# A two-layer graph attention kernel: one sign in eight of two granules made on VectorE, and a new order of work between the layers

## The reference

```python
# layer 1
src = h @ a1; dst = h @ a2
e = leaky_relu(src[:, None] + dst[None, :], 0.01)
e = where(adj > 0, e, NEG_INF)
x = layernorm(x + softmax(e, axis=1) @ h)
# layer 2, on the x of layer 1
wh = x @ weight_w
e = leaky_relu((wh @ a_src)[:, None] + (wh @ a_dst)[None, :], 0.01)
e = where(adj > 0, e, NEG_INF)
x = layernorm(x + softmax(e, axis=1) @ wh + bias)
```

## Time and profile before

| | us |
|---|---|
| median of three runs | 491.33 |
| lowest, highest | 489.75, 494.29 |
| the profiled execution | 490.02 |
| its span, first to last instruction | 487.6 |
| TensorE busy in the span | 435.6 (89%) |
| VectorE busy | 413.6 (85%) |
| ScalarE busy | 394.3 (81%) |
| GpSimd busy | 85.3 (18%) |

### The profile page before, as it was taken

One profiled execution on the slowest core, in us unless ns is written; L12 is line 12 of the kernel. 1 busy time (PEld: TensorE's weight loads), 2 busy tenths in 40 slices (PEclk: granted clock), 3 DMA queues, 4 the chain that ended last, 5 costly groups with the idle time before them and its releaser, 6 DMA issues.

```text
span 487.6 us, 11722 instructions
## 1 busy us (share of the span) xinstructions
PE 435.6 (89%) x4409; PEld 411.8 (84%) x4409; DVE 413.6 (85%) x751; ACT 394.3 (81%) x586; POOL 85.3 (18%) x59
## 2 busy tenths in 40 slices
PE   0799858998988989899998997989999999999993
PEld 0379757987988889899888986989999999999993
DVE  3789998889989898989989997999677786967776
ACT  2685188778897888779889918999999999999940
POOL 0012221512415133151431210001010010101011
PEclk9987979997999979889898988999999999999998
DMA  7999999999999999999994300152130303021100
GB/s 184 255 245 273 273 269 276 330 310 313 326 320 328 308 311 307 311 335 303 321 322 143 130 1 0 58 162 64 36 97 0 97 0 97 11 86 55 42 12 13
DMA packets 83525, 89.27 MB, mean 183 GB/s; under 512 B 7426, under 2 KB 79394, under 8 KB 83490
## 3 DMA queue, kind: packets, MB, share of 16 engines
q1 hardware_dynamic: 48834, 54.57, 39.8%
q10 hardware_dynamic: 34656, 34.21, 25.5%
HBM read 79.32 MB, written 9.45 MB: 182 GB/s over the span
## 4 chain that ended last, share of the span: by engine, by line
PE 42%; DVE 24%; DMA 18%; issue 12%; ACTq 1%; ACT 1%; SPq 1%; POOL 0%; POOLq 0%; DVEq 0%
PE acc L467 40%; DMA stage<-in_adj 17%; DVE narrow L872 5%; DVE turned L884 4%; DVE pos L893 2%; DVE num L987 1%; DMA kept<-in_x 1%; DVE num L994 1%; DVE red L982 1%; DVE kept L794 1%; DVE bn L999 1%; DVE num L984 1%; DVE kept L884 1%; PE flip L393 1%; DVE kept L788 1%
## 5 line engine op out<-in xcount | busy, mean ns | idle before, releaser
L602 ACT ACTIVATE neg<-srow,dcol 128x512 int8<-128x512 f32 (+1 forms) x320 | 222.5, 861 | 11.8 <-issue 8.0
L467 PE MATMUL acc<-xy_old,pos 128*128 128x195 bf16 x1024 | 195.9, 261 | 18.1 <-POOL pos L1143 11.4
L467 PE MATMUL acc<-xy_old,neg 128*128 128x195 bf16 x1024 | 195.7, 261 | 0.0
L467 PE MATMUL acc<-stage,pos 128*128 128x195 bf16 x1024 | 180.6, 250 | 2.6 <-issue 2.6
L467 PE MATMUL acc<-stage,neg 128*128 128x195 bf16 x1024 | 180.5, 250 | 0.0
L602 ACT ACTIVATE neg<-xy_old,dcol 128x512 int8 (+1 forms) x192 | 137.5, 1034 | 0.0
L467 PEld LDWEIGHTS acc<-xy_old,pos 128*128 128x128 fp8e4 x1024 | 106.5, 104 | 26.9 <-issue 25.4
L467 PEld LDWEIGHTS acc<-xy_old,neg 128*128 128x128 fp8e4 x1024 | 105.8, 103 | 1.4
L467 PEld LDWEIGHTS acc<-stage,pos 128*128 128x128 fp8e4 x1024 | 101.7, 99 | 3.4 <-issue 3.0
L467 PEld LDWEIGHTS acc<-stage,neg 128*128 128x128 fp8e4 x1024 | 101.2, 99 | 0.3
L872 DVE TENSOR_SCALAR narrow<-stage 128x4096 uint8<-128x4096 int32 x32 | 74.3, 2320 | 13.1 <-DMA stage<-in_adj 12.2
(11 more groups left out here) (134 smaller groups left out, 345.9 us busy)
## 6 DMA issues: line engine op xcount, KB each, us to landing
stage<-in_adj ACTq DMA_DIRECT2D x64, 512.0 KB, 9.3
stage<-in_adj SPq DMA_DIRECT2D x64, 512.0 KB, 9.2
spill<-turned SPq DMA_DIRECT2D x16, 512.0 KB, 7.7
turned<-spill SPq DMA_DIRECT2D x16, 512.0 KB, 3.7
xy_old<-score_rows SPq DMA_DIRECT2D x6, 256.0 KB, 4.4
out<-x1s SPq DMA_DIRECT2D x7, 128.0 KB, 1.9
xn<-in_x SPq DMA_DIRECT2D x1, 768.0 KB, 16.6
kept<-in_x SPq DMA_DIRECT2D x4, 128.0 KB, 3.9
```

What stands on the lines that cost most here:

```text
L467: last = nc.tensor.matmul(acc[:, r, c * XW:(c + 1) * XW], masks[c][:, t // BYTES, t % BYTES, r * P:(r + 1) * P], xy[layer][:, g * GT + t, ...
L602: last = nc.scalar.activation(o[:, t // BYTES, t % BYTES, :], row, ACT.Sign, bias=dcol[:, layer, col:col + 1])
```

## The change

- VectorE makes tile 7 of granules 1 and 3 of blocks 2 to 7 in layer 2 (`own_sign`): a comparison of the kept row with minus the column score, times 255, written into the same place of `neg`. ScalarE makes seven signs there and eight in granules 0 and 2. `minus_columns` computes the negated scores once. That is 12 comparisons on VectorE and 12 Signs fewer on ScalarE.
- TensorE's order between the layers: (2, 0, 0) is done in two halves, with `project(6)` between them; `score_row(1, 1)` goes behind `turn_x1(7)`; `mean1` goes from ahead of (2, 0, 2) to behind it.
- ScalarE makes the signs of (2, 0, 2) around `copy_x1(7)`, and ahead of `copy_wh(7)`. For this VectorE copies the column scores of supers 4 and 5 early (`columns`).
- `scores1` fills one stretch of PSUM instead of two, and the copy of it is one instruction instead of two.
- VectorE's order in block 1: the read of block 0 goes ahead of mask (1, 1), and mask (1, 2) goes ahead of `add_near` to `moments`. `normalize1(0)` then follows `moments` directly. In the loop the order of the instructions is the same as before, with `own_sign` ahead of the masks of granules 1 and 3, and the loop's seam in another place.

```diff
+    OWN = (None, GT - 1, None, GT - 1)
...
+            granule(1, 0, 0, (0, 1))
+            project(NS - 2)
+            granule(1, 0, 0, (2, 3))
+            turn_x1(NS - 1)
             score_row(1, 1)
-            project(NS - 2)
-            granule(1, 0, 0)
-            turn_x1(NS - 1)
             project(NS - 1)
             turn_max(1)
             spread_max(1)
             granule(1, 0, 1)
             pe.wait_ge(xT_ready, 2 * NS)
-            mean1()
+            pe.wait_ge(shift_ready, 4)
             scores1(NS - 2, NS)
             granule(1, 0, 2)
+            mean1()
...
+                if kept_row and OWN[g] is not None:
+                    tiles = [t for t in tiles if t != OWN[g]]
...
+            signs(1, 0, 2, range(0, 5))
             copy_x1(NS - 1)
+            signs(1, 0, 2, range(5, GT))
             copy_wh(NS - 1)
-            signs(1, 0, 2, range(0, 4))
             act.wait_ge(shift_ready, 4)
             exps(1, slice(NEAR, TILES), minus_shift[:, 1, 0:1], minus_shift[:, 1, 1:2], far_exp)
-            signs(1, 0, 2, range(4, GT))
...
+            def own_sign(s, g):
+                k = (NS + s) * NG + g
+                o = neg[:, g, :].rearrange("p (b i e) -> p b e i", b=GB, e=BYTES)
+                t = OWN[g]
+                dve.wait_ge(products, (k + 1) * RB)
+                dve.sem_inc(dve_turn, 1)
+                row = rows_sb[:, bass.ds(s - 2, 1), :].rearrange("p o n -> p (o n)")
+                nc.vector.tensor_scalar(o[:, t // BYTES, t % BYTES, :], row, minus_dcol[:, g * GT + t:g * GT + t + 1], 255.0,
+                                        ALU.is_lt, ALU.mult).then_inc(own_signs, 1)
+                dve.wait_ge(own_signs, 1 + (s - 2) * (NG // 2) + g // 2 + 1)
...
+            columns(slice(NEAR_SUPS, NS - 2), 2)
             step(weigh(1, 1, rest1))
...
             mask1(1, 0)
             keep_score_rows()
             row_factors1()
+            read_acc(1, 0)
             mask1(1, 1)
-            read_acc(1, 0)
+            mask1(1, 2)
             add_near()
             average(1, 0)
             residual_sum(1, 0)
             moments(1, 0)
-            mask1(1, 2)
             normalize1(0)
+            minus_columns()
+            mask1(1, NG - 1)
...
             with dve.Fori(1, NS - 1) as s:
-                mask1(s, NG - 1)
-                for g in range(NG):
-                    if g:
-                        mask1(s + 1, g - 1)
-                    if g == 1:
-                        read_acc(1, s)
-                    if g == 2:
-                        average(1, s)
-                        residual_sum(1, s)
-                        moments(1, s)
+                mask1(s + 1, 0)
+                read_acc(1, s)
+                mask1(s + 1, 1)
+                average(1, s)
+                residual_sum(1, s)
+                moments(1, s)
+                mask1(s + 1, 2)
                 normalize1(s)
-            mask1(NS - 1, NG - 1)
+                mask1(s + 1, NG - 1)
```

More of the change, by code:

```diff
@@ L150, in gat_kernel @@
         scores = old_f[:, near_end:near_end + IB]
+        minus_dcol = old_f[:, near_end + IB:near_end + IB + TILES]
         raw_near = old_f[:, rows_end:raw_end].rearrange("p (r n) -> p r n", r=RB)
@@ L162, in gat_kernel @@
         s_psum0 = misc[:, 408:408 + IB]
-        s_psum1 = [misc[:, 408:408 + 3 * IB // 4], flip[:, 256:256 + IB // 4]]
+        s_psum1 = misc[:, 408:408 + IB]
         mean_psum = flip[:, 0:BYTES * D]
@@ L204, in gat_kernel @@
         signs_ready = sem("signs_ready")
+        own_signs = sem("own_signs")
         neg_ready = sem("neg_ready")
@@ L407, in scores1 @@
             def scores1(first, end):
-                part = first // (NS - 2)
                 for s in range(first, end):
@@ L411, in scores1 @@
                         b = s * RB + r
-                        last = nc.tensor.matmul(s_psum1[part][:, row_at(s - part * (NS - 2), r)], xT[:, b * P:(b + 1) * P],
-                                                v_src[:, :], start=True, stop=True)
-                if end in (NS - 2, NS):
+                        last = nc.tensor.matmul(s_psum1[:, row_at(s, r)], xT[:, b * P:(b + 1) * P], v_src[:, :],
+                                                start=True, stop=True)
+                if end == NS:
                     last.then_inc(scores_psum, 1)
@@ L591, in signs @@
                     else:
-                        act.wait_ge(dcol_ready, 1 + g // (NG // 2))
+                        act.wait_ge(dcol_ready, max(1, g))
                 act.wait_ge(products, (k + 1) * RB)
@@ L602, in signs @@
                     last = nc.scalar.activation(o[:, t // BYTES, t % BYTES, :], row, ACT.Sign, bias=dcol[:, layer, col:col + 1])
-                if tiles[-1] == GT - 1:
+                if tiles[-1] >= GT - 2 and (kept_row or tiles[-1] == GT - 1):
                     last.then_inc(signs_ready, 1)
@@ L759, in keep_scores @@
             def keep_scores():
-                dve.wait_ge(scores_psum, 4)
-                nc.vector.tensor_copy(scores[:, 0:3 * IB // 4], s_psum1[0])
-                nc.vector.tensor_copy(scores[:, 3 * IB // 4:IB], s_psum1[1]).then_inc(scores_kept, 1)
+                dve.wait_ge(scores_psum, 3)
+                nc.vector.tensor_copy(scores, s_psum1).then_inc(scores_kept, 1)
             def keep_score_rows():
@@ L805, in tables0, with columns @@
                 split(0, g, rest0).then_inc(tables_ready, 1)
+            def columns(supers, n):
+                t = slice(supers.start * BYTES, supers.stop * BYTES)
+                dve.wait_ge(wh_kept, 1 + supers.stop)
+                nc.vector.tensor_copy(dcol[:, 1, t], wh1[:, t, D]).then_inc(dcol_ready, 1)
+                dve.wait_ge(dcol_ready, n)
             def far_columns(n):
                 t = [slice(0, NEAR), slice(NEAR, TILES)][n]
-                dve.wait_ge(wh_kept, 1 + [NEAR_SUPS, NS][n])
-                nc.vector.tensor_copy(dcol[:, 1, t], wh1[:, t, D]).then_inc(dcol_ready, 1)
-                dve.wait_ge(dcol_ready, n + 1)
+                columns([slice(0, NEAR_SUPS), slice(NS - 2, NS)][n], [1, 3][n])
                 nc.vector.tensor_reduce(mcol[:, 4:5], dcol[:, 1, t], AX, ALU.max).then_inc(max_step, 1)
@@ L909, in last_mask0, with minus_columns @@
                 nc.vector.tensor_tensor(c, c, a, ALU.bitwise_and).then_inc(neg_ready, 1)
+            def minus_columns():
+                nc.vector.tensor_scalar(minus_dcol, dcol[:, 1, :], -1.0, None, ALU.mult).then_inc(own_signs, 1)
+            def own_sign(s, g):
[8 more added lines that the diff above has]
+                dve.wait_ge(own_signs, 1 + (s - 2) * (NG // 2) + g // 2 + 1)
             def negative(s, g):
                 k = (NS + s) * NG + g
+                if OWN[g] is not None and not (isinstance(s, int) and s < 2):
+                    own_sign(s, g)
                 dve.wait_ge(signs_ready, k + 1)
@@ L1100, in _ @@
             moments(1, 0)
-            mask1(1, 2)
             normalize1(0)
-            with dve.Fori(1, NS - 1) as s:
-                mask1(s, NG - 1)
-                for g in range(NG):
-                    if g:
-                        mask1(s + 1, g - 1)
-                    if g == 1:
-                        read_acc(1, s)
-                    if g == 2:
-                        average(1, s)
-                        residual_sum(1, s)
-                        moments(1, s)
+            minus_columns()
+            mask1(1, NG - 1)
+            dve.wait_ge(own_signs, 1)
+            for n, rows in enumerate((1, NS - 3)):
+                dve.wait_ge(rows_in[n], 16 * rows)
+            with dve.Fori(1, NS - 1) as s:
+                mask1(s + 1, 0)
[5 more added lines that the diff above has]
+                mask1(s + 1, 2)
                 normalize1(s)
-            mask1(NS - 1, NG - 1)
+                mask1(s + 1, NG - 1)
             for part in HALVES:
```

## The result

The changed kernel takes 494.2 us (median of 17 runs, 492.03 to 496.55), the kernel before in the same comparisons 490.68 us (17 runs). The ratio is 1.0074, 95% interval 1.0054 to 1.0094, which is 3.6 us (2.6 to 4.6) slower. I forecast 2.0 us slower.

A forecast was written before the change was run, and what follows sets the result against it. TensorE was taken to pace blocks 2 to 7, with ScalarE's savings hidden. 490.02 + 0.3 (between the layers and block 1) + 1.7 (loop and tail) = 492.0 us profiled, 493.3 us for the median; range 490.3 to 496.5.

The forecast's parts named there:

- The bound: Layer 2, blocks 2 to 7: TensorE paces at 22.1 us a block, and ScalarE's 8.6 us less work gains nothing.
- ScalarE's pace: Rival, blocks 2 to 7: ScalarE holds TensorE, so 12 fewer Signs bring up to 8.6 us; chance 0.05.
- The 8 us of idle time: Sign of a right forecast: ScalarE idle by some 8 us in blocks 2 to 7.
- Block 1: Layer 2, block 1: stalls of 2.18 and 0.40 us go, a new one of 3.0 us comes ahead of (2, 1, 3).
- GpSimd's power: Block 1, ahead of `normalize1(0)`: the power takes 1.82 us, and VectorE stands still for 2 us.
- TensorE's end of block 0: Layer 2: TensorE ends block 0 at 321.85 as before, with up to 0.4 us more.
- The sum of the whole stretch: Between the layers and through block 1: +0.3 us, from -0.3 at best to +0.8 if the copy is late.
- The comparison: `own_sign` on VectorE in the loop: 0.54 us each, 0.51 for the instruction and 0.03 for the wait until the mask.
- The rival at one element a time: The comparison takes 0.79 us with its wait, so loop and tail cost 3.4 us instead of 1.7; chance 0.12.
- What it exposes: Granule 2's mask, blocks 2 to 7: 0.54 us later against 0.42 slack, so 0.12 us a block exposed, 0.7 in all.
- The clock: Rival: TensorE's clock falls behind the new stall in block 1, costing 1.7 us, to 495.0; chance 0.26.
- Loop and tail: Blocks 2 to 7: 0.7 us for six masks plus 1.0 us ahead of (2, 7, 3), together 1.7 us.

The follow-up runs named there:

- fewer_signs: The kernel before with tile 7's sign left out, not replaced, in granules 1 and 3 of blocks 2 to 7; one execution, 206.3 us from block 6's turn to the end.
- compare_only: The kernel before plus the twelve comparisons, seven Signs in those granules and the moved loop seam, with the old order elsewhere; ratio 1.006.
- after_look1: The changed kernel, unchanged, traced a second time; 210.8 us from the turn of block 6 to the end.
- after_look2: The changed kernel, unchanged, traced a third time; 209.4 us from the turn of block 6 to the end.
- mean_back: The changed kernel with `mean1` put back ahead of (2, 0, 2); ratio 1.0043 to the kernel before.
- mask_first: The changed kernel with the mask of block 1's granule 3 moved ahead of `normalize1(0)` and `minus_columns`; ratio 1.0055 to the kernel before.
- order_only: The changed kernel with no comparison on VectorE and all eight Signs on ScalarE, so only the order differs from the kernel before; ratio 1.0032.
- mask_first_no_compare: The changed kernel with block 1's granule 3 mask ahead of `normalize1(0)` and no comparison on VectorE; ratio 0.9977 to the kernel before.
- before_look1: The kernel before, unchanged, traced a second time; 206.4 us from the turn of block 6 to the end.

## Why the prediction was right or wrong

**The bound: right.** TensorE paces blocks 2 to 7, and ScalarE's 12 Signs fewer are worth nothing there (fewer_signs, compare_only). The rival "ScalarE's pace" is out. The 8 us of idle time I had ScalarE down for came as 2.7 us of waits for TensorE and 4.4 us less from its first Sign of these blocks to its last (133.06 us against 137.47).

**Block 1: the mechanism was right, two sizes were off.** The stalls of 2.18 and 0.40 us went, and one came ahead of (2, 1, 3), released by VectorE's mask. I had 3.0 us, and the three traces show 1.97, 1.49 and 1.50. One size was GpSimd's power: it took 1.01 us instead of the 1.82 of the earlier trace rows, and VectorE waited 1.32 us for it, where I had 2. The other was TensorE's end of block 0, which I had held at its old time. Counted from the turn of block 6 TensorE was ready for block 1 0.4 us later than before in the first trace. There the mask of (2, 1, 2) still waited 0.39 us for ScalarE's Signs, as I had assumed; in the two later traces TensorE ended block 0 so late that the Signs were ready, and the stall was shorter by the difference. The chain of the changed kernel, 335 to 350 us, without its pieces of up to 0.1 us, reads as the list I had written:

```profile
337.56 0.18 DVE small L1029
337.92 1.01 POOL small L1160
339.05 0.20 DVE x1s L1039
339.28 0.75 DVE x1s L1039 x3
340.13 1.14 DVE neg L944
341.29 1.24 DVE pos L949
342.62 7.42 PE acc L469 x84
```

The sum of the whole stretch came to +0.5 us on average (-0.5 to +1.7) for the +0.3 I took, whose range was -0.3 to +0.8. Both ends were missed. At the top is after_look1, which has the low-clock stretch of 1.7 us; after_look2 has it as well and came to +0.3.

**The comparison: 0.516 us measured for 0.51.** The view of the changed line gives least, median and greatest of the twelve in ns:

```profile
L932 DVE TENSOR_SCALAR neg<-xy_old x12: 509/516/525, 348.8 to 472.0; 128x512 uint8 x12
L932 DVEq FUSED_REGOPS  x6: 69/69/69, 348.6 to 460.4; - x6
```

The row for the narrowing of adj, scaled, was the right neighbour. The rival at one element a time is out. The estimate from the Trainium skill, "VectorE: DVE Perf Modes", cycle comparison, 0.42 us, was 0.1 too low; the 0.07 that I had added for the scalar per partition makes up most of that.

**What it exposes: the term that was mis-sized.** I allowed 0.03 us between comparison and mask, as between the two halves of a mask. Behind granule 1's comparison it is 0.13 (348.83 + 0.52 = 349.35 to 349.48), behind granule 3's 0.03 to 0.04. So the mask of granule 2 came 0.65 us later instead of 0.54, and with 0.42 us of slack 0.225 a block were exposed instead of 0.12. For the last granule 3 it is 0.65 + 0.55 = 1.2 instead of 1.08. The six register operations in the rows above stand only at granule 1, once a block. The first begins at 348.6 us, ahead of the comparison at 348.83 and not between it and the mask, so the rows don't show them to be the 0.1 us; its cause stays open.

**The tail: a term that was missing.** 0.34 us come behind the last granule 3. In the changed kernel VectorE pauses between its two statistics instructions in the first half of the last block:

```profile
481.00 0.36 DVE L1026 BATCH_NORM_STATS2 bn<-num 128x6 f32<-128x64 f32 x2
481.86 0.25 DVE L1028 BATCH_NORM_AGGREGATE mv<-bn 128x2 f32<-128x6 f32 x2 [0.51 <-DVE bn L1026]
```

Before, the idle time there was 0.15 us. It is 0.51 in all six traces with two comparisons a block (three of the changed kernel, compare_only, mean_back, mask_first), and 0.15 in before, order_only, fewer_signs and mask_first_no_compare. With one comparison a block it is 0.15 as well, but one normalization behind it is 0.17 longer (0.71 against 0.54). Why, stays open.

**The clock.** I had it fall behind the new stall ahead of (2, 1, 3). It never did, in five traces with such a stall of 1.5 to 2.0 us. It fell in another place, in (2, 0, 2), in two of three traces of the changed kernel. I had called the move of `mean1` one that only carries work from one side to the other. That was wrong in what it leaves between: `scores1`, followed by a wait for VectorE's mask. In the Trainium skill, "TensorE: Matmul & The Clock Gate", part 1, the throttled rate is the default and activity releases it, with which these traces agree (0.62 granted in 309 to 312 us of after_look1, 1.00 in the same stretch of before_look1). But I had weighed it only where I expected a long stall, not where a dense product was taken out.

**The sum.** Loop and tail 2.7 instead of 1.7, between the layers 0.5 instead of 0.3: 3.2 instead of 2.0 from the traces, 3.6 by the medians. That 493.3 came within 0.9 us of the measured 494.2 is in part luck: I counted from 491.33, the median of three executions, and the median of seventeen is 490.68, which hid 0.65 us of the error. The ends of my range also differ by 0.1 to 0.2 us from the sums they are said to come from (490.4 and 496.7), which changes nothing.

## What to carry to other kernels

An engine that is busy all the time isn't the bound if the one behind it never waits; here twelve Signs fewer were worth nothing. Taking work from it may pay once the stalls elsewhere are gone and the engine's lead is used up, but no run here shows that. Before giving a busy engine's work to another, find where the other one waits: the same comparison cost 0.225 us a block behind a read and nothing ahead of it. And when an instruction that waits for a slow partner (here `normalize1` for GpSimd's power) is moved next to what it waits for, something has to be put between them.

## What I had not expected of the hardware

GpSimd's power of the same 128 x 4 tile took 1.82 us in block 0 before and 1.01 in the five traces in which `normalize1(0)` waits for it. The difference is what VectorE does meanwhile: in the first case it was making a mask, in the second it stood still. mask_first differs from the changed kernel only in that the mask lies over the power again, and the power is back at 1.82 (first row `after`, second row mask_first):

```profile
337.91 1.01 POOL L1160 TENSOR_TENSOR small<-small,minus_half 128x4 f32<-128x4 f32 x1 [46.87 <-DVE small L1029]
336.35 1.82 POOL L1160 TENSOR_TENSOR small<-small,minus_half 128x4 f32<-128x4 f32 x1 [46.90 <-DVE small L1029]
```

In the loop, with a mask beside it, it was 1.95.
